# Two-layer cross-attention and expert kernel on one Trainium2 core: one value product per pair of heads for both sequences, and the input's normalisation on GpSimd

## What is computed

```python
def _L0_xattn_ref(q, k, v, Wq, bq, Wo, bo):       # q = layernorm(x), k = v = ctx, 16 heads of 8
    qh, kh, vh = (proj_split(q), proj_split(k), proj_split(v))      # all three by Wq, bq
    scores = einsum('bhqd,bhkd->bhqk', qh, kh) / sqrt(8)
    scores = where(i >= j, scores, -1e10)
    attn = einsum('bhqk,bhkd->bhqd', softmax(scores), vh)
    return attn.transpose(0, 2, 1, 3).reshape(B, S, D) @ Wo + bo
x = x + _L0_xattn_ref(_layernorm(x), ctx, ctx, ...)
x = x + _L0_ffn_ref(_layernorm(x), ...)     # 64 experts, 8 chosen for each token, and a shared one
x = x + _L1_xattn_ref(_layernorm(x), ctx, ctx, ...)   # values rolled by the best lags of a correlation
x = x + _L1_ffn_ref(_layernorm(x), ...)     # ternary weights
```

## Time and profile before

| | us |
|---|---|
| median of three runs | 1315.44 (1314.62 to 1316.75) |
| the profiled execution, whole | 1318.08 |
| its span in the profile | 1316.3 |
| TensorE products busy | 1248.5 (95%) |
| TensorE weight loads busy | 1004.1 (76%) |
| VectorE busy | 1072.9 (82%) |
| ScalarE busy | 920.2 (70%) |
| GpSimd busy | 761.8 (58%) |
| mean granted clock of TensorE | 0.984 |

### The profile page before, as it was taken

How to read it: one execution, slowest core, us unless ns; L and a number is a source line. 1 busy time by engine, 2 the same in 40 slices (tenths; PEclk the granted TensorE clock), 3 DMA queues, 4 the chain that set the end, 5 groups by cost and what they waited for, 6 DMA issues and landing times. The chain is left out here.

```text
span 1316.3 us, 29967 instructions
## 1 busy us (share of the span) xinstructions
PE 1248.5 (95%) x9114; PEld 1004.1 (76%) x9114; DVE 1072.9 (82%) x2050; ACT 920.2 (70%) x1563; POOL 761.8 (58%) x817
## 2 busy tenths in 40 slices
PE   7999999996999999999999999999999999798976
PEld 4777777774788887788878887788888887687865
DVE  4878888885987988978977987978987976578887
ACT  3778888883776776777777776777777776766740
POOL 3765666562565655655665665755665533466770
PEclk9999999997999999999999999999999999999998
DMA  4501010101987686877687676777687683100004
GB/s 119 114 27 32 28 32 28 32 16 32 213 189 171 177 180 149 191 180 168 170 181 178 161 180 152 187 180 175 165 189 177 164 202 81 33 26 25 17 2 128
DMA packets 126150, 159.57 MB, mean 121 GB/s; under 512 B 20840, under 2 KB 59504, under 8 KB 126064
## 3 DMA queue, kind: packets, MB, share of 16 engines
q1 hardware_dynamic: 124974, 158.16, 49.8%
q10 hardware_dynamic: 1090, 0.43, 0.1%
HBM read 152.25 MB, written 6.29 MB: 120 GB/s over the span
## 5 line engine op out<-in xcount | busy, mean ns | idle before, releaser
L1036 DVE TENSOR_TENSOR e_m<-e_pu,raw 128x1024 f32<-128x1024 f32 x256 | 310.0, 1212 | 95.2 <-ACT e_pu L1099 67.6
L1099 ACT ACTIVATE e_pu<-e_pu 128x1024 f32<-128x1024 f32 x256 | 258.6, 1010 | 161.3 <-PE e_pu L1135 159.6
L1109 ACT CAST e_mh<-e_m 128x1024 fp32r<-128x1024 f32 x256 | 268.1, 1047 | 47.0 <-DVE e_m L1036 45.5
L955 POOL TENSOR_TENSOR e_ml<-e_m,e_mh 128x1024 fp32r<-128x1024 f32 x80 | 193.0, 2415 | 125.2 <-ACT e_mh L1109 125.0
L1041 DVE TENSOR_TENSOR e_ml<-e_m,e_mh 128x1024 fp32r<-128x1024 f32 x176 | 238.8, 1357 | 21.6 <-ACT e_mh L1109 20.8
L1133 PE MATMUL e_pu<-r_xh,wuh 128*128 128x512 f32 x528 | 215.4, 408 | 2.6 <-PEq L208 1.9
L1144 PE MATMUL e_py<-e_mh,wdh 128*128 128x512 f32 x528 | 208.7, 395 | 3.0 <-ACT held L1086 3.0
L1134 PE MATMUL e_pu<-r_xh,wul 128*128 128x512 f32 x528 | 209.7, 397 | 0.0
L1135 PE MATMUL e_pu<-r_xl,wuh 128*128 128x512 f32 x528 | 209.6, 397 | 0.0
L1145 PE MATMUL e_py<-e_mh,wdl 128*128 128x512 f32 x528 | 209.4, 397 | 0.0
L1148 PE MATMUL e_py<-e_ml,wdh 128*128 128x512 f32 x528 | 168.4, 398 | 0.9 <-DVE e_ml L1041 0.4
(11 more groups left out here) (229 smaller groups left out, 2397.4 us busy)
## 6 DMA issues: line engine op xcount, KB each, us to landing
raw<-gates_scratch SPq DMA_DIRECT2D x512, 256.0 KB, 4.3
x_res<-in_x_dram SPq DMA_DIRECT2D x64, 64.0 KB, 1.8
xcT<-in_ctxT_dram SPq DMA_DIRECT2D x64, 64.0 KB, 2.0
held<-in_ctx_dram SPq DMA_DIRECT2D x32, 128.0 KB, 2.1
out_dram<-t_res SPq DMA_DIRECT2D x16, 256.0 KB, 2.3
raw<-in_L_ffn_W_up_dram SPq DMA_DIRECT2D x4, 512.0 KB, 4.3
raw<-in_L_ffn_W_down_dram SPq DMA_DIRECT2D x4, 512.0 KB, 5.6
gates_scratch<-raw SPq DMA_DIRECT2D x16, 128.0 KB, 2.3
```

Of the source, the lines that this page charges most:

```text
L955: nc.gpsimd.tensor_tensor(flat(ml[k][:]), flat(m[k][:]), flat(mh[k][:]).bitcast(F32), ALU.subtract).then_inc(m_low[1], 1)
L1036: nc.vector.tensor_tensor(flat(m[r % 3][:]), flat(pu[r % 3][:]), flat(gt[i % SPREAD]), ALU.mult).then_inc(gated, 1)
L1099: nc.scalar.activation(flat(pu[k][:]), flat(pu[k][:]), ACT.Silu).then_inc(silued, 1)
L1109: nc.scalar.copy(flat(mh[k][:]), flat(m[k][:])).then_inc(m_high, 1)
```

## The change

`weigh` makes one product for each pair of heads, for both sequences: all 128 columns of the turned probabilities are the weights, and the 36 columns of vx for the pair (two sequences, two heads, nine each) stream through. The result holds each query's weighed values by its own sequence and by the other one; `invert_sum` and `scale_out` read on each half of the partitions the entries of its own sequence, with two operations each. po takes 288 columns of its bank, po_turned moves behind it, and po_out lies over po. The normalisation leaves VectorE and becomes two operations on GpSimd, a subtraction and a multiplication with a wait between them; the waits that protect its buffers move with it.

```diff
@@ -136,9 +136,9 @@
         ps = psum("ps", [P, 4, 512])[:, :, 0:4 * S].rearrange("p g (h k) -> p g h k", k=S)
         ppT = psum("ppT", [P, 8, P])
         pob = psum("pob", [P, 512])
-        po = pob[:, 0:144].rearrange("p (h d) -> p h d", d=9)
-        po_turned = pob[:, 144:272]
-        po_out = pob[:, 272:400]
+        po = pob[:, 0:288].rearrange("p (j b a d) -> p j b a d", b=2, a=2, d=9)
+        po_turned = pob[:, 288:416]
+        po_out = pob[:, 0:128]
         p_beta = pob[:, 400:401]
         p_bias = pob[0:3, 144:272]
 
@@ -146,6 +146,7 @@
         stats = sem("a_stats_done")
         mean_var = sem("a_mean_var")
         rstd_done = sem("a_rstd_done")
+        centred = sem("a_centred")
         normed = sem("a_normed")
         biased = sem("a_biased")
         turned = sem("a_turned")
@@ -249,18 +250,12 @@
             def _(dve):
                 def stats_of(t, r):
                     at_least(dve, loaded[r], t // 4 * 32 + 32 if isinstance(t, int) else (t - r) * 8 + 32)
-                    wait_apart(dve, rstd_done, 2 * (t - 1), idle["dve"])
+                    wait_apart(dve, normed, t - 1, idle["dve"])
                     nc.vector.bn_stats(st[:, r % 2, :], x_res[:, bass.ds(t, 1), :]).then_inc(stats, 1)
 
                 def aggregate(t, r):
                     wait_apart(dve, stats, 2 * t + 1, idle["dve"])
                     nc.vector.bn_aggr(mv[:, r % 2, :], st[:, r % 2, :]).then_inc(stats, 1)
-
-                def norm(t, r):
-                    at_least(dve, rstd_done, 2 * t + 2)
-                    at_least(dve, turned, t - 1)
-                    nc.vector.tensor_scalar(xn[:, r % 2, :], x_res[:, bass.ds(t, 1), :], mv[:, r % 2, 0:1],
-                                            rstd[:, r % 2, :], ALU.subtract, ALU.mult).then_inc(normed, 1)
 
                 def row_max(t, r):
                     at_least(dve, scored, t + 1)
@@ -275,13 +270,20 @@
 
                 def invert_sum(t, r):
                     at_least(dve, weighed, t + 1)
-                    nc.vector.reciprocal(rden[:, r % 2, :], po[:, :, 8]).then_inc(recip, 1)
+                    for b in range(2):
+                        q = slice(64 * b, 64 * b + 64)
+                        ins = nc.vector.reciprocal(rden[q, r % 2, :].rearrange("p (j a) -> p j a", a=2), po[q, :, b, :, 8])
+                    ins.then_inc(recip, 1)
 
                 def scale_out(t, r):
                     at_least(dve, recip, t + 1)
                     at_least(dve, o_turned, t - 1)
-                    nc.vector.tensor_tensor(o[:, r % 2], po[:, :, 0:8], rden[:, r % 2, :].unsqueeze(2).to_broadcast([P, H, HD]),
-                                            ALU.mult).then_inc(scaled, 1)
+                    for b in range(2):
+                        q = slice(64 * b, 64 * b + 64)
+                        ins = nc.vector.tensor_tensor(o[q, r % 2].rearrange("p (j a) d -> p j a d", a=2), po[q, :, b, :, 0:8],
+                                                      rden[q, r % 2, :].rearrange("p (j a) -> p j a", a=2).unsqueeze(3).to_broadcast(
+                                                          [S, 8, 2, HD]), ALU.mult)
+                    ins.then_inc(scaled, 1)
 
                 def add_out(t, r):
                     at_least(dve, wo_done, t + 1)
@@ -289,7 +291,7 @@
                     nc.vector.tensor_tensor(x_res[:, bass.ds(t, 1), :], x_res[:, bass.ds(t, 1), :], po_out.unsqueeze(1),
                                             ALU.add).then_inc(added, 1)
 
-                order = ((stats_of, 0), (invert_sum, 5), (aggregate, 0), (scale_out, 5), (shift, 3), (norm, 0),
+                order = ((stats_of, 0), (invert_sum, 5), (aggregate, 0), (scale_out, 5), (shift, 3),
                          (add_out, 5), (row_max, 2))
                 turn = in_order(order, n_tiles)
 
@@ -400,6 +402,13 @@
                         nc.gpsimd.tensor_scalar(ve[:, r % 2, :], mv[:, r % 2, 1:2], 1e-5, None, ALU.add).then_inc(rstd_done, 1)
                         at_least(pool, rstd_done, 2 * t + 1)
                         nc.gpsimd.tensor_tensor(rstd[:, r % 2, :], ve[:, r % 2, :], cst["mhalf"][:], ALU.pow).then_inc(rstd_done, 1)
+                        at_least(pool, turned, t - 1)
+                        nc.gpsimd.tensor_tensor(xn[:, r % 2, :], x_res[:, bass.ds(t, 1), :], mv[:, r % 2, 0:1].unsqueeze(1).to_broadcast([P, 1, D]),
+                                                ALU.subtract).then_inc(centred, 1)
+                        at_least(pool, rstd_done, 2 * t + 2)
+                        wait_apart(pool, centred, t + 1, idle["pool"])
+                        nc.gpsimd.tensor_tensor(xn[:, r % 2, :], xn[:, r % 2, :], rstd[:, r % 2, :].to_broadcast([P, D]),
+                                                ALU.mult).then_inc(normed, 1)
                     if live(t, 4, n_tiles):
                         at_least(pool, normed, t - 3)
                         nc.gpsimd.tensor_tensor(x_res[:, bass.ds(t - 4, 1), :], x_res[:, bass.ds(t - 4, 1), :],
@@ -564,9 +573,7 @@
                     at_least(pe, v_out, t + 1)
                     at_least(pe, added, t)
                     for j in range(8):
-                        for b in range(2):
-                            q = slice(64 * b, 64 * b + 64)
-                            ins = nc.tensor.matmul(po[q, 2 * j:2 * j + 2, :], pT[:, r % 2, j, q], vx[:, r % 4, j, b], start=True, stop=True)
+                        ins = nc.tensor.matmul(po[:, j], pT[:, r % 2, j, :], vx[:, r % 4, j], start=True, stop=True)
                     ins.then_inc(weighed, 1)
 
                 def out_project(t, r):
```

## The result

| | before (run beside it) | after |
|---|---|---|
| median, us | 1316.10 | 1393.22 |
| ratio | | 1.0588 (95%: 1.0570 to 1.0606) |
| the profiled execution / its span, us | 1318.1 / 1316.3 | 1393.7 / 1391.4 |
| TensorE products / loads busy, us | 1248.5 / 1004.1 | 1297.3 / 1047.8 |
| VectorE / ScalarE / GpSimd busy, us | 1072.9 / 920.2 / 761.8 | 1116.3 / 921.0 / 810.8 |

The changed kernel is 77 us slower. Nearly all of it lies in the attention: its last add to the residual ends at 387.8 us, at 313.8 before, 74.0 of the 75.1 us that the span grew. The steady loop (window as in the earlier trace rows: length, busy us by engine, clock, DMA share, GB/s) has the full clock, too; products now leave PE idle for 20.5 of 242 us.

The account below looks back on a forecast made before the run. PE was taken to bound the attention at 4.39 us a tile, VectorE close behind. Later weighed values (+0.57) and halves (+0.40) gave, through the circle, +0.93 a tile, 60 us over 64 tiles: 1375 us, range 1355 to 1392.

Parts of the forecast that it names:

- What bounds the kernel: Attention's steady loop: PE at its limit, 4.39 us a tile, VectorE's circle only 0.1 to 0.2 us of slack behind.
- The load: Weighing on PE: 16 loads of 128 columns at 0.112 us each, 1.79 us where 1.05 stand today.
- the term of 0.74 for PE alone: Weighing on PE: +0.74 us a tile, 47 us in all; as a rival by itself 1363, chance 0.14.
- When the weighed values are ready: Between weighing and VectorE's reciprocal: the reciprocal starts at 210.65 instead of 210.08, +0.57 us.
- The halves on VectorE: One reciprocal and one scaling more between weighing and shift, 0.20 us each, +0.40 a tile.
- The circle: Attention tile: the shift starts 0.97 us later but ends in time; PE waits for the scaling; tile +0.93, to 5.32.
- The normalisation: Leaving VectorE gains nothing; on GpSimd it adds 1.0 us a tile without a new wait.
- The sum: Whole attention: 64 tiles at 0.93 us, 60 us more, forecast 1375 us.
- clock: Rival: TensorE's granted clock falls in one attention tile of four, 1398 to 1427 us, chance 0.06.
- rival 5: GpSimd late in the attention, its operations stretched and keys late: 1.2 us a tile, 77 us, 1392; chance 0.04.
- whole halves: Case in the range: VectorE's second halves cost full durations, 1.06 us a tile, 68 us, 1383.

Follow-up runs that it names:

- e1: The changed kernel with one reciprocal and one scaling over all 128 partitions, reading only the first sequence's columns; 1351.8 us, ratio 1.0269.
- e2: The kernel before with only its reciprocal and scaling taken by halves of 64 partitions, product untouched; 1358.9 us, ratio 1.0318.
- e8: The changed kernel with the aggregate ahead of the reciprocals on VectorE; 1381.8 us, ratio 1.0507.
- e10: The changed kernel with the aggregate ahead of the reciprocals and the upper half's scaling ahead of the lower; 1377.2 us, ratio 1.0460.
- e3: The kernel before with a second reciprocal and a second scaling over all 128 partitions, into spare tiles; ratio 1.0074.
- e7: The changed kernel with the normalisation back on VectorE, product and halves as changed; 1392.0 us, ratio 1.0591.
- e6: The kernel before with only the normalisation moved to GpSimd; ratio 1.0034.
- e9: The kernel before with its 16 weighing products reordered, eight of one sequence and then eight of the other; 1347.5 us, ratio 1.0236.

## Why the prediction was wrong, point by point

- **What bounds the kernel.** Right: small slack, each tile pays. e1 and e2 move it by one circle each, e8 and e10 take part of it back.
- **The load.** 0.112 a step was forecast from L746; (1.86 - 0.19) / 15 = 0.111 was measured. The Trainium skill's rule on row groups (TensorE: Matmul & The Clock Gate, Part 3, The mechanism), which would have given 79 us for this part, is refuted here by the rows of L576 itself: the product of 36 columns adds nothing between loads. From the weighing's first load to the next stage's it is 1.70 (214.27 to 215.97), not 1.79: the next stage's load follows the last of the weighing closely, +0.65. With e1's +0.61 a tile the term of 0.74 for PE alone was 0.13 too high, 8 us of its 47.
- **When the weighed values are ready.** Right: +0.51 for 0.57.
- **The halves on VectorE: the step that failed.** "I take what one small operation delays the next" gave +0.40, bounded above by whole durations, 0.53. It measured +0.84. The price would have covered operations like those of the row it came from (e3: +0.25 in all), but the halves start at another partition. Each then costs its whole duration and takes away the overlap on both sides: of the reciprocals, 0.26 + 0.29 to the aggregate instead of 0.24; then the aggregate's step, 0.21 instead of 0.11; of the scalings, 0.30 + 0.33 instead of 0.20. A full duration was therefore no upper bound: the neighbours' overlap had to be added to it. The Trainium skill (Perfetto Trace Analysis, Optimizing Scalar/DVE Operations) says that the half of the profiled latency that acknowledges the write overlaps with the next instruction. The trace agrees that there is an overlap where the first partition stays, but it is about 0.08 of 0.24 to 0.29 us, not half, and where the first partition changes there is none.
- **The circle.** The forecast let the shift end "in time"; with 0.44 more ahead of it, it is the last to be ready (L535 waits 0.22).
- **The normalisation.** No gain on VectorE: right (e7). No cost on GpSimd beyond the tile's growth: right in the changed kernel, in the loop (e7) and in the steps in which e6 loses; with the old product it costs 4.3 us in the early steps (e6).
- **The sum.** e1, which has the normalisation too, is 2.7% and e2 3.2%; together 5.9%, the measured 5.88%. So exact an agreement is partly luck: a steady tile gains 0.61 and 0.73, together 1.34, where both at once give 1.26. Of the rivals none came; clock and GpSimd stayed as forecast in the loop. The 77 us of rival 5 are the measured 77 by chance: its mechanism, GpSimd late, is not there (e7 takes its operations away and is as slow). That rival also set the end of the range; the forecast's own mechanism, with whole halves, ended at 1383, 10 us below the measured time. The direction was right, and so was most of the path; the size rested on a bound for the halves that was too low.

## What to carry to other kernels

Before merging two products on halves of the array into a wide one, look whether they run side by side: count the time from load to load, not the instructions. And splitting a VectorE operation between partitions 0 to 63 and 64 to 127 costs more than a second operation: group what starts at the same partition, or put other work where it waits already.

## What was not expected of the hardware

- VectorE's operations mostly overlap by about 0.08 us when they start at the same partition, whether over 64 or 128, and stand 0.01 to 0.04 apart when the start goes from 0 to 64 or back. The same start is not enough: the aggregate starts at the end of the reciprocal before the change, and the upper scaling of e10, which waits for the upper reciprocal, 0.04 behind it. Four such changes and two more operations made 1.39 us of 0.55; two more operations without a change of start 0.80 (e3). Whether other starts (32, 96) do the same was not tried.
- The order of the same 16 products decides whether the weighing's loads take 1.01 or 1.73 us (e9).
